# Hybrid layer on one core: squares in PSUM, two banks for the early gates, product banks for the first convolution units

## What is computed

```
zxbcdt = hidden_states @ in_proj_w.T            # gate, x, B, C, dt
xBC    = silu(conv4(xBC) + conv_b)
y      = Y_diag + Y_off + D * x                 # chunked scan, 128 heads in 8 groups
y      = y * silu(gate)
var    = mean(y * y) over the 1024 channels of a group
out    = (y * rsqrt(var + eps) * norm_w) @ out_proj_w.T
```

## Time and profile before

| | |
|---|---|
| median of 3 runs | 2179.96 us (2179.29 to 2180.45) |
| the profiled execution | 2181.42 us |
| span in the profile | 2179.7 us |
| PE, DVE, ACT, POOL busy | 92%, 69%, 54%, 50% |
| mean granted clock of TensorE | 0.976 of full speed |
| tap 0 of the first unit (L880), groups 1 to 8 | 69.9, 276.5, 484.3, 692.3, 900.2, 1108.2, 1314.6, 1521.2 us |

### The profile page before, as it was taken

How to read it: one execution, slowest core, us unless ns; L and a number is a source line. 1 busy time by engine, 2 the same in 40 slices (tenths; PEclk the granted TensorE clock), 3 DMA queues, 4 the chain that set the end, 5 groups by cost and what they waited for, 6 DMA issues and landing times.

```text
span 2179.7 us, 39183 instructions
## 1 busy us (share of the span) xinstructions
PE 2003.3 (92%) x11776; PEld 1645.3 (75%) x11776; DVE 1502.7 (69%) x2710; ACT 1178.5 (54%) x2553; POOL 1086.9 (50%) x955
## 2 busy tenths in 40 slices
PE   3899999999999999999999999999998889978997
PEld 2687778778877887788778877877787667765775
DVE  6698589849884977597669757984988551286214
ACT  2596368537843874396449636953784225321441
POOL 1288149705951693179228814971596025330423
PEclk7899999999999999999999999999999999999999
DMA  2452035114411341233134203511351149923894
GB/s 83 127 154 85 20 117 162 48 42 121 155 49 60 110 138 40 85 119 103 40 89 151 82 26 107 164 57 33 125 160 29 59 163 383 326 60 111 295 386 141
DMA packets 143908, 261.75 MB, mean 120 GB/s; under 512 B 19536, under 2 KB 35920, under 8 KB 143696
## 3 DMA queue, kind: packets, MB, share of 16 engines
q1 hardware_dynamic: 134848, 231.35, 32.8%
q0 software_dynamic: 7520, 24.65, 3.5%
q10 hardware_dynamic: 1328, 3.15, 0.4%
HBM read 233.38 MB, written 25.69 MB: 119 GB/s over the span
## 4 chain that ended last, share of the span: by engine, by line
PE 31%; DVE 31%; issue 23%; POOL 11%; ACT 2%; DVEq 1%; DMA 1%; another core or an unknown queue 1%; POOLq 0%; ACTq 0%; SPq 0%
PE bank L1470 20%; DVE Y L1184 7%; PE bank L1753 5%; POOL Y L702 4%; DVE Y L1193 3%; PE bank L1765 3%; DVE mem L1172 2%; DVE cv L1230 2%; DVE E L1215 2%; DVE mem L1152 2%; DVE Y L1209 2%; POOL wl L685 2%; POOL mem L678 1%; POOL mem L664 1%; DVE gt L1221 1%
## 5 line engine op out<-in xcount | busy, mean ns | idle before, releaser
L1470 PE MATMUL bank<-xh,wh 128*128 128x512 f32 x1288 | 525.9, 408 | 31.4 <-DVE quad L1193 13.3
L1470 PE MATMUL bank<-xh,wl 128*128 128x512 f32 x1288 | 505.3, 392 | 0.0
L1470 PE MATMUL bank<-xl,wh 128*128 128x512 f32 x1288 | 503.3, 391 | 0.0
L685 POOL TENSOR_TENSOR wl<-raw,wh 128x512 fp32r<-128x512 f32 x144 | 184.5, 1286 | 518.9 <-ACT wh L862 518.9
L1470 PEld LDWEIGHTS bank<-xh,wh 128*128 128x128 f32 x1288 | 243.3, 189 | 88.2 <-DVE quad L1193 20.4
L1184 DVE SCALAR_TENSOR_TENSOR Y<-bank,cpar,Y 128x511 f32<-128x511 f32 (+2 forms) x384 | 287.0, 747 | 31.6 <-ACT Y L880 22.6
L1470 PE MATMUL bank<-wh,ah 128*128 128x512 f32 x576 | 235.6, 409 | 54.2 <-DVE al L1233 27.5
L1470 PEld LDWEIGHTS bank<-xh,wl 128*128 128x128 f32 x1288 | 242.6, 188 | 54.2
L1470 PEld LDWEIGHTS bank<-xl,wh 128*128 128x128 f32 x1288 | 243.8, 189 | 45.3 <-issue 0.5
L702 POOL TENSOR_TENSOR Y<-Y,gt 128x512 f32<-128x512 f32 x128 | 197.1, 1542 | 83.7 <-DVE gt L1221 83.7
L1233 DVE TENSOR_TENSOR al<-Y,ah 128x512 fp32r<-128x512 f32 x128 | 105.3, 828 | 188.9 <-ACT ah L933 188.9
(11 more groups left out here) (214 smaller groups left out, 3963.1 us busy)
## 6 DMA issues: line engine op xcount, KB each, us to landing
mem<-c_rows SPq DMA_DIRECT2D x128, 256.0 KB, 3.7
mem<-wffn_d SPq DMA_DIRECT2D x62, 512.0 KB
E<-e_rows SPq DMA_DIRECT2D x256, 96.0 KB, 3.4
raw<-wconv_d SPq DMA_DIRECT2D x80, 256.0 KB, 2.7
cv<-c_rows SPq DMA_DIRECT2D x64, 256.0 KB, 4.1
spare<-c_rows SPq DMA_DIRECT2D x64, 256.0 KB, 4.0
raw<-wgate_d SPq DMA_DIRECT2D x64, 256.0 KB, 2.7
raw<-wout_d SPq DMA_DIRECT2D x64, 256.0 KB, 2.6
```

Source lines behind the costliest of these rows:

```text
L685: inc(pool.tensor_tensor(wl[:, W_SLOT[p], :], raw[:, R_SLOT[p], :], wh[:, W_SLOT[p], :], ALU.subtract), w_lo)
L1470: got = mm(out, l, r, start=first and n == 0, stop=last and n == 2)
```

## The change

It gives the squares from gate 2 on a place in PSUM: bank 0 for n = 2 to 7 (one buffer), banks DG and OF in turn for n = 8 to 15. The `sq` buffers in SBUF go, and with them ACT's wait for `ss_add` before the first unit. A list `BANKS` replaces k mod 3: products 0, 1, 2 take ST, OF, DG; 3 to 19 take banks 1, 2, 0 in turn; gates 0 to 7 (products 20 to 27) take banks 1 and 2 in turn; gates 8 to 15 take 1, 2, 0 in turn, output blocks t mod 3. Product 30, the first to take bank 0 after the squares, waits for the sixth addition (gate 7). DVE adds squares ahead of its gate multiplication in a tick, not behind it. The slots of the output weights are given in another order, and the last piece moves from tick 36 to 35, behind the gate's work of that tick on ACT and DVE.

```diff
-        sq = quad[:, 0, :].rearrange("p (n s) -> p n s", n=2)
+        def sq(n):
+            return bank[SQ_BANK if n < SQ_LATE else (DG, OF)[n % 2]][:, :]
-        W_SLOT = [0, 1, 2, 3, 4, 5, 6, 7, 8, 9, 2, 3, 4, 5, 0, 1, 8, 9, 2, 3, 4, 5, 6, 7, 10, 8]
+        W_SLOT = [0, 1, 2, 3, 4, 5, 6, 7, 8, 9, 2, 3, 4, 5, 0, 1, 8, 9, 6, 7, 10, 2, 3, 4, 5, 8]
-            + [28, 29, 30, 31, 32, 33, 34, 36]
+            + [28, 29, 30, 31, 32, 33, 34, 35]
+        SQ_BANK, SQ_LATE = 0, 8
+        BANKS = [ST, OF, DG] + [(k - 2) % 3 for k in range(3, NCONV)] \
+            + [1 + n % 2 if n < SQ_LATE else (n - SQ_LATE + 1) % 3 for n in range(NGATE)] + [t % 3 for t in range(TT)]
         def big_bank(k):
-            return k % 3
+            return BANKS[k]
         def big_bank_free(eng, i, k):
-            q, wait = (k - 3, now) if k >= 3 else (max(q for q in range(NBIG) if q % 3 == k), before)
+            if k < 3:
+                before(eng, (s_ok, off_ok, ydiag_ok)[k], i, UNITS)
+                before(eng, ss_add, i, NGATE - BATCH)
+                return
+            if k == NCONV + SQ_LATE + 2:
+                now(eng, ss_add, i, SQ_LATE - BATCH)
+                return
+            same = [q for q in range(NBIG) if BANKS[q] == BANKS[k]]
+            q, wait = (max(q for q in same if q < k), now) if min(same) < k else (max(same), before)
...
# ACT, tick k: weights (all but the last piece), unit work, tanh of gate k, then
+                    if k == W_TICK[PIECES - 1]:
+                        weight_hi(PIECES - 1)
...
# ACT, square of gate n = k - 22
-                        if n >= 2 * BATCH:
-                            now(act, ss_add, i, n - 2 * BATCH + 1)
-                        dst = sq[:, n % 2, :] if tile else acc[:, b, :]
+                        if n == BATCH:
+                            now(act, conv_ok, i, NCONV - 2)
+                        elif BATCH < n < SQ_LATE:
+                            now(act, ss_add, i, n - BATCH)
+                        elif n >= SQ_LATE + 2:
+                            now(act, ss_add, i, n - 2 - BATCH + 1)
+                        elif n == SQ_LATE:
+                            now(act, ydiag_ok, i, UNITS)
+                        elif n == SQ_LATE + 1:
+                            now(act, off_ok, i, UNITS)
+                        dst = sq(n) if n >= BATCH else acc[:, b, :]
...
# DVE, tick k: the addition of gate k - 23 now stands ahead of the multiplication of gate k - 20
+                        inc(TTn(acc[:, b, :], acc[:, b, :], sq(n), ALU.add), ss_add)
                     if NCONV <= k < NCONV + NGATE:
...
-                        inc(TTn(acc[:, b, :], acc[:, b, :], sq[:, n % 2, :], ALU.add), ss_add)
+                    if k == W_TICK[PIECES - 1]:
+                        out_weight_lo(PIECES - 1)
...
# PE, states of unit 0
-                            before(pe, s_ok, i, UNITS)
+                            now(pe, conv_ok, i, 3)
```

More of the change, by code:

```diff
@@ L829, in _, with weight_hi @@
             with act.Fori(0, GROUPS) as i:
+                def weight_hi(p):
+                    raw_arrived(act, i, p)
+                    w_slot_free(act, i, p)
+                    kt = p - (PIECES - XT)
+                    if kt == 0:
+                        act.wait_ge(gpar_in, 16 * (i + 1))
+                    scale = gpar[:, kt:kt + 1] if kt >= 0 else 1.0
+                    inc(nc.scalar.activation(wh[:, W_SLOT[p], :], raw[:, R_SLOT[p], :], ACT.Copy,
+                                             scale=scale), w_hi)
                 for k in range(NBIG + 4):
@@ L852, in _ @@
                             inc(nc.scalar.activation(L[n % LR], L[n % LR], ACT.Exp, scale=-1.0), decay_ok)
-                    for p in range(PIECES):
+                    for p in range(PIECES - 1):
                         if W_TICK[p] == k:
[L856 to L863, removed]
+                            weight_hi(p)
                     if k < NCONV:
@@ L875, in _ @@
                             before(act, tr_mm, i, 4)
-                            before(act, ss_add, i, NGATE - BATCH)
                         elif tile == 1:
@@ L1132, in _, with out_weight_lo @@
             with dve.Fori(0, GROUPS) as i:
+                def out_weight_lo(p):
+                    kt = p - (PIECES - XT)
+                    now(dve, w_hi, i, p + 1)
+                    inc(STT(wl[:, W_SLOT[p], :], raw[:, R_SLOT[p], :], gpar[:, kt:kt + 1],
+                            wh[:, W_SLOT[p], :], ALU.mult, ALU.subtract), wo_lo)
                 for k in range(NBIG + 4):
-                    for p in range(PIECES - XT, PIECES):
+                    for p in range(PIECES - XT, PIECES - 1):
                         if W_TICK[p] == k:
[L1137 to L1140, removed]
+                            out_weight_lo(p)
                     u = k - (B_ - 1)
@@ L1216, in _ @@
                                 ALU.mult), off_ok)
+                    n = k - 3 - NCONV
+                    if BATCH <= n < NGATE:
+                        b = GATES[n][1]
+                        now(dve, sq_ok, i, n + 1)
+                        if n > BATCH:
+                            now(dve, ss_add, i, n - BATCH)
+                        inc(TTn(acc[:, b, :], acc[:, b, :], sq(n), ALU.add), ss_add)
                     if NCONV <= k < NCONV + NGATE:
```

## The result

The changed kernel takes 2194.37 us (median of 6 runs, 2184.44 to 2202.19) against 2180.25 us (2179.29 to 2184.57): a ratio of 1.0057, interval 1.0029 to 1.0085. Forecast were 2189 us and a slowdown. Timed again beside other kernels it had 2193.38 us (12 runs) against 2182.84, ratio 1.0044 (1.0030 to 1.0058).

The account below looks back on a forecast made before the run. PE, busy 92% of the span, was taken as the bound, leaving its idle time and clock. Waits of -0.7 and clock of +1.8 made +1.1 us a group, 8.8 for eight: 2189 us, range 2167 to 2204.

Parts of the forecast that it names:

- First units: Start of a group: waits before products 3 and 5 go, product 10 starts earlier; 1.5 us saved a group.
- Product 20: First gate product: with two banks it waits for DVE's reading of unit 18; 3.25 us lost a group.
- units 13 and 14: PE's waits for POOL at these units end inside the stall at product 20; 2.5 us saved a group.
- Gates 22 to 29: Products 22 to 29, gates 2 to 9: DVE's multiplication of two gates before comes early enough; 0 us.
- Product 30: Takes bank 0 and waits for the addition of gate 7 behind a chain over ACT, DVE, POOL; 4.9 us lost.
- Tail: Output blocks 0 and 1: DVE catches up, so PE's waits there mostly go; 4.8 us saved a group.
- Turn of the loop: Between groups: PE's 0.65 us wait hangs on its own last block and stays; 0 us.
- Clock: One fall each at products 20 and 30, at 1.4 us, less 1.0 for the tail's falls: 1.8 us lost a group.
- the clock stays: Rival: no clock falls at products 20 and 30; 1.7 us saved a group, 2166 us, faster; chance 0.28.
- A cheap product 30: Rival: DVE's split gets ahead of POOL, product 30 waits 3.4 us; 2177 to 2180 us, same; chance 0.15.
- The tail does not recover: Rival: DVE stays about a tick late, only 2.4 of 4.8 us come back; 2208 us, slower; chance 0.07.

Follow-up runs that it names:

- Experiment 1: Kernel before with products 0, 1, 2 in banks ST, OF, DG and later ones in banks 1, 2, 0 in turn; squares stay in SBUF: 2161.67 us, ratio 0.9902.
- experiment 2: Kernel before with the change's whole list of banks, early gates on banks 1 and 2 alone; squares stay in SBUF: 2185.31 us, ratio 1.0008.
- experiment 3: Kernel before with only the squares of gates 2 to 15 moved to PSUM, into the idle transpose banks 3 and 5: 2147.32 us, ratio 0.9816.
- experiment 5: Changed kernel with squares in the idle transpose banks 3 and 5, and the early gates on three banks again: 2124.15 us, ratio 0.9739.
- experiment 4: Changed kernel with squares in the idle transpose banks 3 and 5, early gates still on banks 1 and 2: 2145.56 us, ratio 0.9840.
- experiment 7: Changed kernel with DVE's addition of squares also ahead of the output weight's split in a tick: 2166.30 us, ratio 0.9927.

## Why the prediction was right

The sign, the size and the places were right: +8.8 us forecast, +9.7 and +11.6 us in the mixer of two profiles, +10.5 and +14.1 us by the two pairs of medians. By its steps, each for a group:

- **First units, -1.5:** the first tap to that of unit 10 took 34.5 us and takes 33.0. Experiment 1 shows it alone. The waits left, 0.48 and 0.20 us, were given as 0.6 and 0.18.
- **Product 20, +3.25, and units 13 and 14, -2.5:** measured 3.05 us by the modelled ends (3.32 by starts, behind the 0.23 that always lies between matmuls, so 3.1), and no wait at the units. Together with the first units the tanh of gate 7 was to come 0.8 us earlier; it comes at 129.6 for 130.4. The other cover, DVE's states ahead of unit 19, was sized right too: L1223 of unit 19 ends at 582.70, and product 21 starts without a wait.
- **Gates 22 to 29, 0:** no wait. The cover was as thin as stated: experiment 2, where the long addition is still in the way, loses 0.74 us at product 28.
- **Product 30, +4.9:** 4.76 us, 4.92 from the time when the next product was due. The split that meets POOL took 1.18 and 1.19 us.
- **Tail, -4.8:** no wait over 0.1 us is left. From product 35's tanh to the `ah` of block 2 it takes 8.4 us; 12.67 before without a fall and 14.25 with one. With the 0.5 us that the late gates gain, this is 4.7.
- **Turn of the loop, 0:** the prediction had it hang on PE's own last block and stay. In both kernels most turns wait for POOL's split of the next group's weight, and the mean over seven turns goes from 0.73 to 0.87 us: about 1 us in all that was put at nothing. Why it grows stays open.
- **Clock, +1.8:** the term came out near (+1.7 and +1.9 in the two profiles), its two parts did not. The step was "one fall for each, at 1.4 us". At product 20 the first profile has falls in two of eight groups, the second in three, not in all: 0.4 and 0.6 us a group. At product 30 a fall comes in all sixteen, in fourteen of them about twice as long: from the tanh of gate 9 to that of gate 10 it takes 9.9 us, where 2.7 and the wait of 4.9 make 7.6, so 2.3 us. Less the 1.0 of before this gives the term. What failed is the number of falls at product 20, which was too high, and the price of one at product 30, which was too low. That the two errors cancel is luck: the right total does not show that the clock was understood.

The rival "the clock stays" was wrong at product 30 and mostly right at product 20. "A cheap product 30" was wrong: the splits do come behind POOL. "The tail does not recover" was wrong; experiments 3 and 5 show that the squares in SBUF were what made DVE late and that banks of PSUM cure it without a stall, though experiment 2 suggests that a stall alone brings part of it.

The change so holds three gains (first units, squares off SBUF, DVE's order) and pays for their place with two waits on banks, one of which the clock charges again in every group and the other in some. The places were the fault: with the squares in banks that are idle anyway (experiment 5) the same gains make 56 us, 2.6%.

What stays open: why the clock falls behind product 20 in all groups of experiments 4 and 7, in seven of eight of experiment 2 and in two or three of the changed kernel, with 3.0 us of wait in each. And the first pair of medians lies 4 us over the mixer's 9.7, which was not located; the experts' scatter is larger than that.

## What to carry to other kernels

When a buffer moves to PSUM to keep DVE from waiting for POOL, look for a bank that is idle in just these ticks before taking one from a ring: a ring of three cut to two makes the first product behind a stage change wait for the slowest reader of the stage before. When one product waits for a consumer chain, write that chain out across engines in program order: here two weight splits that had nothing to do with it were 2.7 of 4.8 us. And count an added wait of PE with the clock it may cost, which at product 30 was about half as much again (2.3 us for 4.9).

## What the runs showed of the hardware that was not expected

- A fall of the clock about twice as long behind one wait: 4.7 to 5.4 us of work at 1.2 GHz behind a wait of 4.76 us, 2.3 to 2.6 us lost, in seven of eight groups of the first profile; in the eighth the wait was the same and the loss 1.5 us.
- Waits equal to 0.05 us in every group, and yet falls behind the tail in five of the eight groups of the kernel before and in one of experiment 1. The cause is not shown.
- The addition of two inputs in SBUF took 5.56 us where POOL ran five instructions without a pause, and ended 0.54 us behind the last of them (the first row below), in all eight groups. This does not always happen: the next two additions took 1.19 us each, the second of them (last row) ended 0.55 us behind the first of two back-to-back instructions of POOL and ahead of the end of the second, so it waited for one of them alone. What sets the two cases apart was not tested. With one input in PSUM it took 0.672 to 0.689 us in all 112 cases.

```profile
611.95 1.31 POOL L702 TENSOR_TENSOR Y<-Y,gt 128x512 f32<-128x512 f32 x1
...
616.05 3.45 POOL L702 TENSOR_TENSOR Y<-Y,gt 128x512 f32<-128x512 f32 x2
...
617.16 1.19 DVE L1230 TENSOR_TENSOR cv<-cv,quad 128x512 f32<-128x512 f32 x1
```
